# Scores with keys on partitions and a maximum over the copies in SBUF, in a perceiver layer on one core

## The reference

```python
q = (norm(x) @ Wq + bq); k = ctx @ Wk + bk; v = ctx @ Wv + bv       # 16 heads x 64
logits = einsum('bshd,bShd->bhsS', q, k) / 8
x = x + softmax(logits) @ v @ Wo + bo                               # cross attention
qkv = norm(x) @ qkv_w.T + qkv_b                                     # 16 heads x 32, scaled by head_mask
x = x + (softmax(q @ k.T / sqrt(32)) @ v) @ fc_w.T + fc_b           # self attention
h = norm(x); rw = softmax over the chosen experts of l2norm(h) @ l2norm(sim) - sigmoid(gates)
q, k, v = einsum('btc,ech,bte->bth', h, proj_e, rw)                 # 16 experts each
x = x + sum_e rw_e * (causal_softmax(q @ k.T / sqrt(128)) @ v) @ o_proj_e
```

## Time and profile before

| | |
|---|---|
| median of 3 runs | 1469.93 us (1469.12 to 1470.01) |
| profiled execution | 1469.58 us, span 1467.8 us |
| DMA | 78.3 MB, mean 53 GB/s |
| instructions | 22757 |

### The profile page before, as it was taken

One profiled execution on the slowest core, in us unless ns is written; L12 is line 12 of the kernel. 1 busy time (PEld: TensorE's weight loads), 2 busy tenths in 40 slices (PEclk: granted clock), 3 DMA queues, 4 the chain that ended last, 5 costly groups with the idle time before them and its releaser, 6 DMA issues.

```text
span 1467.8 us, 22757 instructions
## 1 busy us (share of the span) xinstructions
PE 1417.4 (97%) x8628; PEld 1119.6 (76%) x8628; DVE 759.2 (52%) x1784; ACT 493.4 (34%) x1113; POOL 198.8 (14%) x164
## 2 busy tenths in 40 slices
PE   6999999999999999999999999999999887799999
PEld 5877788778777877787777777877887666678877
DVE  6445533463355335533443464345435556877769
ACT  4235521561155116412531373135214624222210
POOL 2321100220020003100100140011000233300030
PEclk9999999999999999999999999999999998799999
DMA  6511100240020004201100150021001320113300
GB/s 215 187 40 34 30 12 0 78 128 12 1 80 12 12 11 137 69 0 46 35 23 1 54 145 19 1 61 30 11 1 44 112 88 30 58 58 117 101 13 29
DMA packets 45817, 78.33 MB, mean 53 GB/s; under 512 B 6688, under 2 KB 14912, under 8 KB 44688
## 3 DMA queue, kind: packets, MB, share of 16 engines
q1 hardware_dynamic: 44192, 72.38, 15.9%
q0 software_dynamic: 1520, 4.51, 0.9%
HBM read 71.63 MB, written 5.24 MB: 52 GB/s over the span
## 4 chain that ended last, share of the span: by engine, by line
PE 92%; DVE 4%; ACT 1%; issue 1%; DMA 1%; POOL 0%; SPq 0%; ACTq 0%; DVEq 0%
PE b_ps L1121 25%; PE b_ps L1099 25%; PE b_ps L479 9%; PE b_ps L1168 8%; PE b_ps L1137 8%; PE b_ps L1150 7%; PE b_ps L505 3%; PE b_ps L410 3%; PE b_ps L1109 2%; PE b_ps L1191 1%; PE b_ps L415 1%; DMA b_raw_v<-in_Wv 1%; ACT b_ctxT L1227 0%; PE b_ps L1161 0%; ACT t_prob L549 0%
## 5 line engine op out<-in xcount | busy, mean ns | idle before, releaser
L1121 PE MATMUL b_ps<-b_ctxT,wk 128*128 128x512 f32 x1536 | 390.0, 402 | 0.0
L1099 PE MATMUL b_ps<-wv,b_ctxT 128*128 128x512 f32 x1536 | 368.1, 398 | 12.0 <-DVE b_ctxT L1325 12.0
L1099 PEld LDWEIGHTS b_ps<-wv,b_ctxT 128*128 128x128 f32 x1536 | 288.1, 189 | 85.3 <-issue 19.9
L1121 PEld LDWEIGHTS b_ps<-b_ctxT,wk 128*128 128x128 f32 x1536 | 281.5, 188 | 86.8 <-issue 25.0
L1302 ACT COPY b_pT<-b_ps 128x512 f32<-128x512 f32 x128 | 74.9, 585 | 604.1 <-PE b_ps L1150 603.4
L1431 DVE COPY b_pT<-b_ps 128x512 f32<-128x512 f32 x128 | 88.3, 690 | 254.8 <-PE b_ps L1150 254.6
L1343 DVE COPY b_V<-b_ps 128x512 f32<-128x512 f32 x128 | 88.4, 691 | 239.6 <-PE b_ps L1099 239.6
L1293 ACT ACTIVATE b_prob<-b_prob,b_negm 128x512 f32<-128x512 f32 x256 | 183.0, 720 | 58.1 <-DVE b_negm L1452 58.1
L1446 DVE TENSOR_SCALAR_CACHE_REDUCE b_prob<-b_ps 128x512 f32<-128x512 f32 x256 | 166.5, 688 | 29.7 <-PE b_ps L1137 28.1
L1059 POOL TENSOR_TENSOR wk<-stage,wk 128x512 fp32r<-128x512 f32 x30 | 38.9, 1296 | 761.0 <-ACT wk L1235 761.0
L1150 PE MATMUL b_ps<-ident,b_prob 128*128 128x128 f32 x1024 | 133.0, 272 | 3.9 <-DVE b_pT L1431 3.6
(11 more groups left out here) (197 smaller groups left out, 1126.1 us busy)
## 6 DMA issues: line engine op xcount, KB each, us to landing
stage<-in_ctx SPq DMA_DIRECT2D x64, 256.0 KB, 2.9
b_wo<-in_Wo SPq DMA_DIRECT2D x8, 1024.0 KB, 6.4
stage<-in_Wk SPq DMA_DIRECT2D x30, 256.0 KB, 2.6
stage<-in_Wv SPq DMA_DIRECT2D x28, 256.0 KB, 3.2
b_q<-q_s SPq DMA_DIRECT2D x32, 128.0 KB, 3.1
stage<-in_self_w SPq DMA_DIRECT2D x16, 256.0 KB, 3.0
t_raw<-in_q_proj SPq DMA_DIRECT2D x16, 256.0 KB, 4.4
t_raw<-in_k_proj SPq DMA_DIRECT2D x16, 256.0 KB, 3.3
```

The source lines that it names most:

```text
L1099: mm = nc.tensor.matmul(ps[:, G.bank[item]], ctxT[:, a, k, n * P:(n + 1) * P], wv[:, w, k], start=m == 0, stop=m == len(terms) - 1)
L1121: mm = nc.tensor.matmul(ps[:, G.bank["k", t]], wk[:, i % 2, w, k], ctxT[:, a, k, s * BANK:(s + 1) * BANK], start=m == 0, stop=m == len(ter ...
```

## The change

In the cross part:
- `scores(t-1)` now has the keys on partitions of the result: 128 key columns of K are stationary and the 128 queries of q move, 4 blocks x 2 heads, one plain fp32 product each (no high and low parts of q and K any more, so the second K operation and the query remainders go).
- No transposes of probabilities: V is weighted directly by them. L1150 and its copies L1302, L1431 go.
- ScalarE copies both heads' scores of a step out of PSUM in one operation (1024 elements); probabilities live in a ring of five units of two steps.
- The maximum over keys is taken by VectorE from these copies: a running elementwise maximum over the pair (`max_step`), two halvings (`max_end`), then on TensorE two transposes (`turn_top`, in step 4i+5), a row maximum on VectorE (`max_rows`), and on TensorE two matmuls that spread it over the partitions (`spread_top`, step 4i+6). VectorE subtracts it from each unit (`below_max`, 2048 elements), ScalarE takes the exponential of 2048 elements at once. One maximum serves a query of a head over all keys, as before.
- Row sums: a running elementwise sum on VectorE (`sum_step`, `sum_end`), then matmuls with ones; the reciprocal is taken after them.
- The key and value ring has four banks. The lag of weighting stays 8, value and output products come two steps later, the context chunks of a batch are split from one step earlier, behind the key and score copies.

In self attention GpSimd's normalisation, head mask, bias addition and three weight remainders are VectorE's; low parts have items of their own (`xl`, `al`, `hl`, `wl`), so the list places them; the square root by iteration uses per column scalars in two operations a round instead of three; the list is written anew.

```diff
-    LAG_EXP, LAG_TURN, LAG_WEIGH = 5, 6, 8
+    LAG_WEIGH, RING = 8, 4
-                self.products[half * h + 5 + n // SB].append(("v", h, n))
+                self.products[half * h + 7 + n // SB].append(("v", h, n))
-    BY_POOL = (0, 1, 2, 13, 14, 15)
+    BY_POOL = (13, 14, 15)
...
-                    pe.wait_ge(s_out, 2 * t)
-                for m, (l, a) in enumerate(((0, 0), (1, 0), (0, 1))):
+                    pe.wait_ge(s_out, t)
+                for c in range(SB):
                     for h in range(2):
                         rows = slice(h * HD, (h + 1) * HD)
-                        mm = nc.tensor.matmul(ps[:, SCB + h], q[rows, i % 2, l], kst[rows, t % 2, a], start=m == 0, stop=m == 2)
+                        mm = nc.tensor.matmul(ps[:, SCB + h, c * P:(c + 1) * P], kst[rows, t % 2, c * P:(c + 1) * P], q[rows, i % 2],
+                                              start=True, stop=True)
...
+            def turn_top(i):
+                pe.wait_ge(mx_done, i + 1)
+                pe.wait_ge(sub_done, 2 * i)
+                for h in range(2):
+                    mm = nc.tensor.transpose(ps[:, MB, h * P:(h + 1) * P], mx[:, h, 0], ident[:])
+                mm.then_inc(turn_psum, 1)
+            def spread_top(i):
+                pe.wait_ge(m_done, i + 1)
+                for h in range(2):
+                    mm = nc.tensor.matmul(ps[:, MB, (2 + h) * P:(3 + h) * P], tops[:, i % 2, h:h + 1].broadcast_to([P, P]), ident[:],
+                                          start=True, stop=True)
...
-                            nc.tensor.matmul(ps[h * HD:(h + 1) * HD, OB, P:2 * P], rinv[:, i % 2, h:h + 1].broadcast_to([P, HD]),
-                                             ident[:], start=False, stop=True, skip_group_check=True)
+                            nc.tensor.matmul(ps[h * HD:(h + 1) * HD, OB, P:2 * P], ones[:], total[:, h],
+                                             start=False, stop=True, skip_group_check=True)
...
+                    nc.scalar.copy(prob[:, unit % UNITS, :, s * SB:(s + 1) * SB], ps[:, SCB:SCB + 2].rearrange("p h (c t) -> p h c t", c=SB)
+                                   ).then_inc(s_out, 1)
+                unit = 2 * ((t - SB - 3) // SB) + (t + 1) % SB
+                if t % SB in (3, 0) and 0 <= unit < 2 * NB * NP:
+                    act.wait_ge(sub_done, unit + 1)
+                    p = prob[:, unit % UNITS]
+                    nc.scalar.activation(p, p, ACT.Exp, scale=SCALE).then_inc(exp_done, 1)
...
+            def max_step(i, s):
+                so_far = blocks(2 * i, 0) if s == 1 else mx[:]
+                nc.vector.tensor_tensor(mx[:], blocks(2 * i + s // 2, s % 2), so_far, ALU.max).then_inc(top_done, 1)
...
+            def below_max(i, a):
+                top = ps[:, MB, 2 * P:].rearrange("p (h t) -> p h t", h=2)[:, :, None].broadcast_to([P, 2, UC, P])
+                nc.vector.tensor_tensor(p, p, top, ALU.subtract).then_inc(sub_done, 1)
...
+                if r == 0 and i - 2 in pairs:
+                    sum_step(i - 2, 1)
+                if r == 0 and i - 1 in pairs:
+                    max_step(i - 1, 3)
+                    max_end(i - 1)
+                if r == 1 and i - 3 in pairs:
+                    attention_out(i - 3)
+                if r == 1 and i - 1 in pairs:
+                    max_rows(i - 1)
+                if r == 1 and i - 2 in pairs:
+                    sum_step(i - 2, 2)
+                    sum_step(i - 2, 3)
+                if r == 2 and i - 1 in pairs:
+                    below_max(i - 1, 0)
+                if r == 2 and i in pairs:
+                    max_step(i, 1)
+                if r == 2 and i - 1 in pairs:
+                    below_max(i - 1, 1)
+                if r == 3 and i - 2 in pairs:
+                    sum_end(i - 2)
+                if r == 3 and i in pairs:
+                    max_step(i, 2)
```

More of the change, by code:

```diff
@@ L141, in __init__ @@
         ring = [x for x in self.first if x[0] == "v"]
-        banks, last = deque(range(3)), {}
+        banks, last = deque(range(self.RING)), {}
         self.bank, self.earlier, self.nth, self.unit, counts = {}, {}, {}, {}, {}
@@ L149, in place @@
                 place_one(y)
+        ends = {"sx": "xl", "sw": "al", "sh": "hl"}
         at = {x: n for n, x in enumerate(self.rest)}
+        at.update({x: at[ends[x[0]], x[1]] for x in self.rest if x[0] in ends})
         def place_one(x):
@@ L187, in __init__ @@
         work += [(half * h - 6 + c, ("wv", h, c)) for h in range(1, self.HALVES) for c in range(C)]
-        work += [(self.STEPS * b - 3 + n // 4 + n % 4 // 2, ("ctx", b, n)) for b in range(1, NB + 1) for n in range(NC)]
+        work += [(self.STEPS * b - (4 if b < NB else 3) + n // 2 - n // 6, ("ctx", b, n)) for b in range(1, NB + 1) for n in range(NC)]
         work.sort(key=lambda w: (w[0], ("ctx", "wk", "wv").index(w[1][0]), w[1]))
@@ L600, in root, with wide_root @@
     def root(self, dve, x, y, part):
-        V, E = self.nc.vector, x.shape[-1]
-        bits, near, minus = self.bits[:, :E], self.near[:, :E], self.minus[:, :E]
-        if part == 0:
-            V.tensor_scalar(minus, x, -0.5, None, ALU.mult)
-            self.step(dve, V.tensor_scalar(bits, x.bitcast(I32), 1, None, ALU.logical_shift_right))
-            self.step(dve, V.tensor_scalar(y.bitcast(I32), bits, -1, 0x5F3759DF, ALU.mult, ALU.add))
-        else:
+        V, columns = self.nc.vector, [slice(n, n + 1) for n in range(x.shape[-1])]
+        bits, near, minus = self.bits, self.near, self.minus
+        if part == 0:
+            V.tensor_scalar(minus[:, :len(columns)], x, -0.5, None, ALU.mult)
+            self.step(dve, V.tensor_scalar(bits[:, :len(columns)], x.bitcast(I32), 1, None, ALU.logical_shift_right))
+            self.step(dve, V.tensor_scalar(y.bitcast(I32), bits[:, :len(columns)], -1, 0x5F3759DF, ALU.mult, ALU.add))
+        else:
+            for c in columns:
+                ins = V.tensor_scalar(near[:, c], y[:, c], y[:, c], minus[:, c], ALU.mult, ALU.mult)
+            self.step(dve, ins)
+            for c in columns:
+                ins = V.tensor_scalar(y[:, c], near[:, c], 1.5, y[:, c], ALU.add, ALU.mult)
+            self.step(dve, ins)
+    def wide_root(self, dve, x, y):
+        V, E = self.nc.vector, x.shape[-1]
+        near, minus = self.near[:, :E], self.minus[:, :E]
+        self.root(dve, x, y, 0)
+        for _ in range(3):
             self.step(dve, V.tensor_tensor(near, y, y, ALU.mult))
@@ L728, in vector @@
             dve.sem_inc(self.out[kind], 1)
[L729 to L730 removed]
+            self.wide_root(dve, self.sims[:], self.simn[:])
             self.step(dve, V.tensor_scalar(self.simn[:], self.simn[:], Z.D ** -0.5, None, ALU.mult))
+        elif kind == "gn":
+            self.norms(dve, item)
         elif kind == "gl":
+            self.gate_logits(dve, item)
+        elif kind == "gt":
             self.gating(dve, item)
@@ L737, in vector @@
             self.use_product(dve, item)
-        elif kind == "wt" and item[1] not in self.BY_POOL:
+        elif kind == "wl" and item[1] not in self.BY_POOL:
             m = item[1]
```

450 lines of the change are left out of this document (207 added, 243 removed).

## The result

The new kernel takes 1422.36 us (median of 4 runs, 1421.5 to 1422.41) against 1469.53 before (4 runs): ratio 0.968, 95% interval 0.966 to 0.970. That is 47 us less; I had forecast 66 less. The profiled execution took 1422.4 us with a span of 1420.6. First from its page, busy time by engine and the chain that ended last.

The account below looks back on a forecast made before the run. Cross attention was taken as bound by TensorE issue, self attention by a chain between engines. 1469.6 - 63 (TensorE terms) + 6 (waits) - 6 (drain) - 3 (self attention) = 1403.6, forecast 1404 us; 8 in 10 range 1369 to 1440.

Parts of the forecast that it names:

- term 1: Cross attention on TensorE: the transposes of the probabilities go, saving 116 us (bounds 95 to 124).
- term 2: Cross attention scores on TensorE: the new matmul form takes 1.11 us a step, +0.21, adding 27 us.
- term 3: Cross attention: the maximum crosses TensorE by transposes and matmuls, 0.80 us a pair, adding 26 us (bounds 22 to 38).
- Waits in the cross part: Cross attention: TensorE's new waits, for the maximum's crossings and at batch boundaries, add 6 us (0 to +25).
- the spare time of 1.3 us: First crossing of the maximum in cross attention: about 1.3 us to spare when neither ScalarE nor VectorE is late.
- the drain: End of cross attention: old transpose waits and a slow stretch go, short maximum waits come; -6 us (0 to -10).
- Self attention: Self attention: work moved from GpSimd to VectorE, set against stalls and waits removed; -3 us (bounds -15 and +12).
- The late maximum: Cross attention rival, chance 0.13: the maximum arrives late in every pair, +48 us, giving 1452.
- The row halves rival: Cross attention scores, chance 0.03: row halves do not overlap, 1.94 us a step, +106 us, giving 1510.
- the bound on VectorE: Cross attention rival, chance 0.03: VectorE becomes the bound at about 27 us a pair, +128 us, giving 1532.
- the 45 below which I would have called the forecast wrong: Cross part: the forecast is wrong if it loses less than 45 us or more than 95.
- The crossings' waits: Sign: TensorE's waits on VectorE for the maximum's two crossings should total below 10 us.

Follow-up runs that it names:

- e3_transposes: New kernel with three key and value banks instead of four and eight unread transposes a step ahead of the scores; 1523.13 us (1420.68 with three banks alone).
- e1_serial: New kernel with scores issued as one row half's four products first, then the other's; 1480.34 us, ratio to before 1.007.
- e5_nomax: New kernel with the maximum turned and spread only for the first pair, all other pairs subtracting that one; 1399.48 us.
- e8_late: New kernel with the last maximum of each pair computed three times over, same result; 1486.97 us.
- e4_drain: New kernel with the last 12 chunks of the self attention weights split two steps later; 1415.97 us.
- e11_order_end: New kernel with later self attention weight splits, no chunk remainders on GpSimd, and ScalarE and VectorE work reordered for the last pair only; 1416.12 us.
- e12_all: e11_order_end with the last pair but one's output ahead of VectorE's weight remainders and self attention's work back on GpSimd; 1406.01 us, ratio to before 0.956.
- e9_gpsimd: New kernel with self attention's normalisations, masks, bias additions and three weight remainders back on GpSimd, in the new list order; 1413.88 us.

## Why the prediction was right, and where it was wrong

*Transposes, term 1* (-116): right; e3_transposes prices them at 0.85 a step, 106 to 108 for 126 steps. *Scores, term 2* (+27): right, 1.09 against 0.90 a step is +24 for 128. e1_serial shows that the order of issue is the reason. The rule of the Trainium skill that I used for this term (TensorE: Matmul & The Clock Gate, "The mechanism"), that a weight load overlaps with running products only where the row groups differ, agrees with this pair of kernels too: the same 16 loads and products take 1.09 us with the row groups in turn and 1.64 one group after the other.

*Maximum, term 3* (+26): 0.67 a pair, 21; e5_nomax gave 20. I had counted changes of form that the keys in front pay anyway.

*Waits in the cross part* (+6): 8.3 us against 2.7 for the scores before, so about right, but the spare time of 1.3 us on which it rested holds only in quiet pairs; the mean is 0.4 (e8_late). Counted by what each loop holds, transposes of 121 steps are -117, scores of 126 steps +24, keys of 127 steps at 2.99 for 2.88 +14, crossings +21, the weighting of V that went to the drain -2, waits +6. That gives -55 (unrounded); the loop lost 56.3.

*The step that failed is the drain* ("-6 us (0 to -10)", and with the drain's share of the transposes about -11): it measured +9.5. I counted there only the chain copy, maximum, halvings against one V weighting, as if both engines were free: waits of 1.4 us before the transposed maximum and 0.7 at the second crossing. They were 6.90 and 2.83, and a third of 3.91 for the sums came to them. The trace shows what I left out: four splits, an exponential and a cast queued on ScalarE ahead of the last copy (3.4 us late), a sum step of 1.58 ahead of the last maximum, GpSimd's operation beside the last halving (1.37 instead of 0.43), VectorE's whole share of a pair (two subtractions 4.5, sums, ends), which no key product covers any more, and the slow clock behind the waits. I had booked the slow stretch of the earlier trace rows (3.28 for 32 V instructions) as gone; there is one again (3.31). VectorE was busy for 23.5 of 47 us there before (1142 to 1189) and 43.1 of 56 after (1086 to 1142). e4_drain gave back 4.7 us by the order alone; e5_nomax, e11_order_end and e12_all show that taking away one wait makes another. How much the four slots alone hold, with more slots, was not tried.

*Self attention* (-3, bounds -15 to +12): -0.2, in the bounds, but not for the reasons given. I had set the move against the stalls and waits that it removes. The waits did not go: 13.6 us for GpSimd became 14.8 for VectorE, and with GpSimd back in e9_gpsimd they are 12.0. The move costs 6 to 8, the rest of the edit gains about as much. That the two cancel is luck. The stalls of the earlier trace rows are gone in e9_gpsimd as well, where GpSimd works 38 us and the 128x1 operations average 274 ns; so not GpSimd's absence alone took them away. Whether it was their new form (one tensor input and per partition scalars) or their new place in the list, no run tells apart.

*Rivals.* The late maximum happened in the drain and not in every pair. The row halves rival and the bound on VectorE did not come. VectorE's rows of a pair add up to 16.6 us where I had 15.4 (the reciprocal is 0.7 of the difference), and it was 61% busy in 100 to 1050; in the pair shown above, beside a batch boundary, it was busy for 20.6 of 21.0 us.

*Signs.* The cross part, loop and drain, lost 46.8 us, just beyond the 45 below which I would have called the forecast wrong. The crossings' waits are 14.9 us and not below 10, of which 5.0 lie in the loop.

## What to carry to other kernels

Work that is hidden in a loop comes out at its end: when work moves to another engine, price the last round by itself, with all that is queued on every engine, and not only the steady pair. A gain that rests on products running beside each other is a property of the order in which they are issued; swapping two loops took all of it away. And when the removal of one wait brings the next, look for what may stand behind both (here perhaps the slots and VectorE's work) before changing the order again.
